# A decoder layer on one core: the first batch's output projection moved wholly into the loop

## What is computed

```
proj = layernorm(x) @ W_in.T ; u, gate = split(proj)          # 2048 channels each
u = silu(conv4(u) + conv_b) ; dt, B, C = rmsnorm parts of u @ Wx.T
delta = softplus(dt @ Wdt.T + dt_bias)
for t: state = exp(delta_t*A)*state + (delta_t*u_t)*B_t ; y_t = sum_n(state*C_t)   # 16 states n
y = (y + u*D) * silu(gate)
x = x + y @ W_out.T
```

## Time and profile before

| | us |
|---|---|
| median of 3 runs (lowest, highest) | 1678.84 (1677.64, 1682.73) |
| the profiled execution: its own time | 1682.06 |
| its span | 1680.3 |
| DVE busy | 1314.7 (78%) |
| PE busy | 1413.9 (84%), modelled |
| mean granted TensorE clock | 0.937 of 2.4 GHz |

### The profile page before, as it was taken

How to read it: one execution, slowest core, us unless ns; L and a number is a source line. 1 busy time by engine, 2 the same in 40 slices (tenths; PEclk the granted TensorE clock), 3 DMA queues, 4 the chain that set the end, 5 groups by cost and what they waited for, 6 DMA issues and landing times. The chain is left out here.

```text
span 1680.3 us, 17931 instructions
## 1 busy us (share of the span) xinstructions
PE 1413.9 (84%) x5576; PEld 730.5 (43%) x5576; DVE 1314.7 (78%) x1633; ACT 934.4 (56%) x1378; POOL 936.9 (56%) x771
## 2 busy tenths in 40 slices
PE   6998677788888987768798788888989994999798
PEld 3443234444444453344454454444434442444443
DVE  6586698898898889989998898889147556777684
ACT  1211567767767755877767767755233222556670
POOL 0000778798797877889988898797100000333200
PEclk9999798999998999977999999999999996999899
DMA  7596233442443423343673682674473103589504
GB/s 273 201 346 260 76 132 103 152 163 100 155 157 107 166 84 119 98 141 101 224 246 113 229 279 86 227 231 157 149 284 145 61 25 95 135 190 195 113 0 175
DMA packets 155468, 264.38 MB, mean 157 GB/s; under 512 B 76560, under 2 KB 94096, under 8 KB 149552
## 3 DMA queue, kind: packets, MB, share of 16 engines
q1 hardware_dynamic: 151056, 236.27, 43.7%
q10 hardware_dynamic: 4320, 27.00, 4.5%
HBM read 207.60 MB, written 38.60 MB: 147 GB/s over the span
## 5 line engine op out<-in xcount | busy, mean ns | idle before, releaser
L1047 DVE TENSOR_TENSOR_SCAN hbuf<-decay,hbuf 128x512 f32<-128x512 f32 x512 | 611.7, 1211 | 51.6 <-ACT decay L763 51.6
L763 ACT ACTIVATE decay<-delta,chan_sb 128x512 f32<-128x512 f32 x512 | 348.7, 687 | 293.1 <-DVE hbuf L1047 291.9
L579 PE MATMUL turn<-ident,hbuf 128*128 128x128 f32 x2048 | 337.9, 294 | 179.3 <-DVE hbuf L1047 137.6
L579 PEld LDWEIGHTS turn<-ident,hbuf 128*128 128x128 f32 x2048 | 256.3, 150 | 451.2 <-DVE hbuf L1047 213.7
L1061 DVE SCALAR_TENSOR_TENSOR acc<-turn,pn,acc 128x512 f32<-128x512 f32 x360 | 263.0, 731 | 40.4 <-PE turn L579 39.6
L893 POOL TENSOR_TENSOR hbuf<-du,sx 128x512 f32<-128x512 f32 x172 | 213.1, 1273 | 1.3 <-DMA sx<-bt_scratch 1.3
L893 POOL TENSOR_TENSOR hbuf<-wout,sx 128x512 f32<-128x512 f32 x172 | 213.6, 1278 | 0.4 <-POOL wout L903 0.2
L914 POOL TENSOR_TENSOR acc<-acc,part 128x512 f32<-128x512 f32 x120 | 153.3, 1278 | 52.5 <-ACT part L773 52.3
L1742 PE MATMUL bank<-codes,wout 128*128 128x512 bf16 (+1 forms) x704 | 153.8, 382 | 1.0 <-PEq L1156 1.0
L561 PE MATMUL bank_g<-wout,codes 128*128 128x512 f32 x256 | 139.8, 634 | 2.4 <-DVE wout L993 2.4
L493 PE MATMUL bank_u<-wout 128*128 128x512 f32 x224 | 113.1, 625 | 2.9 <-DMA wout<-in_wu 2.0
(11 more groups left out here) (212 smaller groups left out, 2124.0 us busy)
## 6 DMA issues: line engine op xcount, KB each, us to landing
wout<-in_woutT SPq DMA_DIRECT2D x48, 512.0 KB, 4.3
sx<-bt_scratch SPq DMA_DIRECT2D x86, 256.0 KB, 3.6
codes<-in_wg SPq DMA_DIRECT2D x8, 2048.0 KB, 8.9
ubuf<-u_scratch SPq DMA_DIRECT2D x16, 1024.0 KB, 6.1
wout<-in_w_gate SPq DMA_DIRECT2D x26, 512.0 KB, 4.7
wout<-in_w_up SPq DMA_DIRECT2D x26, 512.0 KB, 4.1
raw_d<-in_w_down ACTq DMA_DIRECT2D x8, 1376.0 KB, 7.4
b_more<-bt_scratch SPq DMA_DIRECT2D x42, 256.0 KB, 3.4
```

The costliest lines, as they stand in the source:

```text
L579: last = pe.transpose(turn[t % 2][:, j * P:j * P + P], hbuf[:, s % 4, j, t * P:t * P + P], ident[:, :])
L763: act.activation(decay_bank[q % 2][:, :], delta[:, G % 2, j, :], ACT.Exp, scale=a_col(GD * (G % GROUPS) + j, n)).then_inc(dA_done, 1)
L1047: dve.tensor_tensor_scan(h, decay_bank[q % 2][:, :], h, 0.0, ALU.mult, ALU.add).then_inc(scan_done, 1)
```

## The change

Tile w of the projection runs in group 4+w rather than 5+w, so all four tiles are in the loop and `wout_last`, the last `wout_copy` and its stores go. In groups 5 to 7 the chunks keep their steps (two in each of 0 to 7), with another w. In group 4 the 16 chunks stand in steps 9 to 14, as 2, 3, 3, 2, 3, 3, and ACT copies them out at the end of step 15. To make room, the gate products of group 4 move from steps 8 to 15 (four in each) to steps 2 to 8 (five in each, two in the last), and their copies from the steps (11, 13, 15, 16) to (3, 5, 6, 8). The weights of the gates are asked for in step 0 rather than 1.

```diff
+        def wout_chunks(G, n):
+            if G < GROUPS:
+                return range(0)
+            if G > GROUPS:
+                return range(2 * n, 2 * n + 2) if n < 8 else range(0)
+            i = n - 9
+            return range(DC * i // 6, DC * (i + 1) // 6) if 0 <= i < 6 else range(0)
+
+        def wout_copied(G, n):
+            return G == GROUPS and n == 15 or G > GROUPS and n == 9
...
-            lo, per = (9, 3) if G == 0 else (5, 3) if G == GROUPS - 1 else (8, 4)
+            lo, per = (9, 3) if G == 0 else (5, 3) if G == GROUPS - 1 else (2, 5) if G == GROUPS else (8, 4)
...
-            at = (-1, -1, 13, 15) if G == 0 else (9, 12, 14, 16) if G == GROUPS - 1 else (11, 13, 15, 16)
+            at = (-1, -1, 13, 15) if G == 0 else (9, 12, 14, 16) if G == GROUPS - 1 else \
+                (3, 5, 6, 8) if G == GROUPS else (11, 13, 15, 16)
... SP
-                    if n == 1 and G >= 1:
+                    if n == (0 if G == GROUPS else 1) and G >= 1:
                         load_wg(G)
...
-                    if b == 1 and g >= 1 and n < 8:
-                        if n == 0:
-                            load_yT(g - 1)
-                        for q in (2 * n, 2 * n + 1):
-                            load_w(BATCH * DC + DC * (g - 1) + q)
-                    if b == 1 and g >= 1 and n == 9:
+                    for c in wout_chunks(G, n):
+                        if c == 0:
+                            load_yT(g)
+                        load_w(BATCH * DC + DC * g + c)
+                    if wout_copied(G, n):
                         for half in range(2):
-                            store_attn(g - 1, half)
+                            store_attn(g, half)
...
-                        load_yT_last()
...
-            for half in range(2):
-                store_attn(TT - 1, half)
-            for i in range(2):
-                sp.wait_ge(yT_stored[i], 16 * (GD * NG // 2))
-            sp.wait_ge(attn_stored, 32 * TT)
+            for part in range(3):
+                sp.wait_ge(wout_in[part], 16)
... PE
-                            pe.wait_ge(wout_evac, 2 * (G - GROUPS))
+                            pe.wait_ge(wout_evac, 2 * (G - GROUPS + 1))
...
-                        pe.wait_ge(gate_evac, TT * (GROUPS + w + 1))
+                        pe.wait_ge(gate_evac, TT * (GROUPS + max(w, 1)))
...
-                        if b == 1 and g >= 1 and n < 8 and t % 2 == 1:
-                            wout_part(g - 1, 2 * n + t // 2, 2 * n + t // 2 + 1)
+                        w = wout_chunks(G, n)
+                        wout_part(g, w.start + len(w) * t // TT, w.start + len(w) * (t + 1) // TT)
...
-            wout_last(KC, DC)
             for j in range(GD):
                 turn_y(NG - 1, j)
-            wout_last(0, KC)
... ACT
-                    if b == 1 and g >= 1 and n == 9:
-                        wout_copy(g - 1)
+                    if G > GROUPS and wout_copied(G, n):
+                        wout_copy(g)
...
                     for j in gate_copies(G, n):
                         gate_copy(G, j)
+                    if G == GROUPS and wout_copied(G, n):
+                        wout_copy(0)
...
-            wout_copy(TT - 1)
```

More of the change, by code:

```diff
@@ L98, in mixer @@
         o_stage = [xT[:, 4, 0:L], xT[:, 5, 0:L]]
-        yT_last = [delta[:, 0, c // 4, (c % 4) * P:(c % 4) * P + P] for c in range(DC)]
         skip_diag = [soft[:, j // 2, (j % 2) * P:(j % 2) * P + P] for j in range(GD)]
-        o_last = [soft[:, half, :] for half in range(2)]
         x_view = [hbuf[:, i // 2, 2 * (i % 2):2 * (i % 2) + 2, :].rearrange("p a t -> p (a t)")
@@ L203, in mixer @@
         EARLY_GATE = 2
-        WOUT_BESIDE = GROUPS - 1
+        def wout_chunks(G, n):
[7 more added lines that the diff above has]
+            return G == GROUPS and n == 15 or G > GROUPS and n == 9
         UNITS = 2 * OC
@@ L346, in store_y @@
                     .then_inc(yT_stored[i % 2], 16)
[L348 to L352, removed]
             def load_yT(w):
@@ L366, in store_attn @@
                 sp.dma_start(attn_dram[w * P:w * P + P, half * 512:half * 512 + 512],
-                             (o_stage if w < WOUT_BESIDE else o_last)[half])\
+                             o_stage[half])\
                     .then_inc(attn_stored, 16)
@@ L438, in _ @@
                         sp.wait_ge(q_step, 4 * UNITS)
-                        sp.wait_ge(w_used, BATCH * DC + DC * WOUT_BESIDE)
+                        sp.wait_ge(w_used, BATCH * DC + DC * TT)
                         sp.wait_ge(dbu_done, GD * N * (NG - 1))
                         load_wout(KC, DC, 0)
-                        load_yT_last()
             sp.wait_ge(gate_mm, TT * NG)
-            sp.wait_ge(attn_stored, 32 * WOUT_BESIDE)
+            sp.wait_ge(attn_stored, 32 * TT)
             load_wout(0, KC // 2, 1)
@@ L609, in wout_part @@
                                          start=(c == 0), stop=(c == DC - 1))
[L610 to L624, removed]
                     last.then_inc(w_used, 1)
@@ L800, in wout_copy @@
             def wout_copy(w):
-                act.wait_ge(w_used, BATCH * DC + (DC * (w + 1) if w < WOUT_BESIDE else DC * w + 1))
+                act.wait_ge(w_used, BATCH * DC + DC * (w + 1))
                 if w >= 1:
@@ L804, in wout_copy @@
                 for half, bank in enumerate((bank_u, bank_s)):
-                    o = (o_stage if w < WOUT_BESIDE else o_last)[half]
-                    act.activation(o, bank[:, :], ACT.Copy).then_inc(wout_evac, 1)
+                    act.activation(o_stage[half], bank[:, :], ACT.Copy).then_inc(wout_evac, 1)
             for i in range(TT):
```

## The result

| | before | after |
|---|---|---|
| median of 4 runs each (us) | 1678.48 | 1698.08 |
| lowest, highest | 1677.64, 1682.73 | 1696.14, 1710.12 |
| ratio, with its 95% interval | | 1.0123 (1.0085 to 1.0161) |
| the profiled execution: time, span | 1682.06, 1680.3 | 1698.34, 1696.6 |
| mean granted TensorE clock | 0.937 | 0.931 |

The kernel is 19.6 us slower. The direction was right, but the projection in groups 4 and 5 was priced too low, and the gain at the end too high.

What follows compares the result with a forecast made beforehand. DVE was taken to pace the loop and PE the mixer's end; end -13.4, copies +10.3, ring +7.5, group 5's start +1.8, PE's clock +1.5 made +7.7 us: 1689.8 profiled, 1686.5 by the median, range 1674 to 1698.

Steps and rivals of the forecast that it cites:

- the gain at the end: After the loop: without wout_last's products the next block starts earlier, -13.4 us, between -15.4 and -10.
- The ring: Group 4: W_out chunks in two places, each turning in 6.2 us, finish late; +7.5 us, bounds +1.5 and about +17.
- the order on SP: Start of group 5: yT and first chunk loads stand behind tile 0's stores; +1.8 us, between 0 and +4.
- PE's own work: Group 4's three-chunk steps: four turns and six products, 7.0 us, alone cost about half a us each.
- The copies: Group 4: ACT's gate bank copies wait for PE and delay decays; +10.3 us in sum, between +5 and +13.
- Bank 2: Step 4.7: the copy delays decays and a softplus, so the next step begins 11.3 after the start, not 7.2; +4.1.
- bank 0: Group 4: PE's step 3 starts 1.3 late and the copy holds the scan 2.3 more; +3.6 us.
- bank 3: Group 4: copy and decay end 6.5 into the step against 3.9, with a softplus in that step too; +2.6 us.
- the rival at 1700: Group 4: PE's waits keep it at 1.2 GHz through the three-chunk steps, two such costing 14 more; 1700, chance 0.15.
- The no-change rival: Group 4: the ring turns within the steps, so its +7.5 goes unpaid; +0.2, 1679; chance 0.18.
- The faster rival: The end keeps 15.4, copies cost at most 5, loads land in about 3.4; -9, 1670; chance 0.15.
- the signs named: Profile after: ACT's gate waits, long steps 4.7 and 4.9, PE's W_out waits, group 4 130 to 135, end 27 not 42.

Runs made afterwards that it cites:

- e12: e3 with 14 of tile 0's 32 products left out and all chunk loads kept; ratio 0.9905 to the kernel before.
- e2: The changed kernel with four places for the chunks of W_out instead of two; 1681.8 us.
- e3: The changed kernel with gate copies one step later, four W_out chunk places, and tile 0's stores behind group 5's first loads; 1664.6 us, ratio 0.9909.
- e5: The changed kernel with tile 0's two stores asked for behind group 5's loads of yT and first chunks; 1693.44 us.
- e4: The kernel before with only the gate part of the change (group 4's gate products and copies earlier), projection as before; 1690.27 us.
- e9: e3 with three unread products added behind the first and three behind the third turn of y after the loop; ratio 0.9928.
- e7: e3 with four banks and four places for y after the loop; 1659.65 us, ratio 0.9897.
- e10: e7 with the 4 MB of W_out at the end left out but for two blocks; tail 27.7 us, no total given.
- e11: e7 with the 4 MB of W_out asked for behind the four stores of y; tail 36.5 us, no total given.

## Why the prediction was wrong

**The step that failed** is the price of the projection in group 4 and at the start of group 5: +7.5 and +1.8 forecast, +15.5 measured. The ring and the order on SP are there, the one priced too high and the other too low; PE's own work was put at next to nothing.

- *PE's own work.* The step said that four turns and six products, 7.0, "alone would cost about half a us each", and then priced the ring. It left out the dt product that PE's steps 4.9 and 4.11 hold as well, and that no gap is left when every step is full. e12 shows 3.1 us of it. Another 1.7 goes from e2 to e3 (47.5 to 45.8, clock 0.90 to 0.96), all of it in steps 4.14 and 4.15; in 4.14 the clock was 0.77 in e2 and 1.00 in e3. That the clock is its whole cause is not shown, since e3 has two more edits. The sum by window would have said so: 35.2 of PE before, less the 24 gate products that leave (20.7), plus 27.6, is 42.1 in a stretch of 41.9; e3 shows 41.99 [its window above]. PE, not DVE, bounds those steps.
- *The ring.* Forecast +7.5 by a turn of 6.2, measured 3.7 (e2). The loads landed in 3.7 there, not in the 4.3 of the earlier trace rows, and PE waited for seven chunks in the stretch, 4.5 in all, in four of its steps 4.10 to 4.14 (not in 4.12) and not in all five. With 3.7 the formula gives 8 x 5.6 = 44.8 for 41.0, +3.8. So that +7.5 came near the +9.3 was luck: too much for the ring, next to nothing for PE.
- *Group 5.* The order on SP was named, and "about 4 us late, mostly beside ACT's silu" was wrong twice: 7.3 late, and nothing hid it. Step 5.1 lost 4.4 and step 5.0 1.8. e5 gives 3.2 of the 6.2 to the order; most of the rest goes when tile 0 ends in time as well (+0.7 in e3). This is the largest single miss, 4.4.

**The second miss** is the end: -13.4 forecast, -9.7 measured. "The other three follow at 2.70 each as now" carried over a distance that was measured at 2.4 GHz and with stores that landed in 2.3. It is 13.95 for the three and not 8.1, 5.9 more. With the clock up in the second turn the three still take 12.5 to 14.4 (e12, e9, e2), since the first store is late; with four banks and places, where neither counts, 2.9 (e7).

**The copies** were right: +10.3 forecast, +10.9 alone (e4), +13.2 in the profile of the whole change. Bank 2 came out at +4.2 (4.1 forecast), bank 0 at +4.0 (3.6) and bank 3 at +4.2 (2.6); with the gates alone it was 4.2, 3.6 and 3.4. Bank 3 was dearer with PE's clock down behind the wait in step 4.7 (1.92 a pair at 775.36); that this is the whole reason is not shown.

**The rivals.** The measured 1698 lies nearest to the rival at 1700, held at 0.15, but its reason did not happen: in steps 4.10 to 4.15 the clock was 0.91, not 0.5. The no-change rival took the ring for free; with the ring of four the kernel does come to 1.0015, but because groups 6 and 7 get 10 shorter: PE's own work, which no rival had at the full clock, is still there. The faster rival needed copies at 5 or less; they cost 10.9. The Trainium skill's estimate (DMA: Bandwidth & Descriptors, Anatomy of one DMA), 3.2 for such a load and by it a free ring, was weighed and set aside. The page gives its figures for DMAs issued by GpSimd, and these are issued by SP, so it did not quite bear on them. The median landing of 3.7 in that stretch lies between it and 4.3, and the ring cost 3.7 us and not nothing.

Of the signs named: ACT's waits for gate products 14.2 in steps 4.3, 4.6 and 4.8 (at least 6) yes; steps 4.7 and 4.9 at 11.3 and 11.8 (10 to 11) just over; PE's waits for W_out in five of the steps 4.10 to 4.14 no, in four; group 4 at 137.4 (130 to 135) over; groups 5 to 7 within 3 us no, group 5 took 6.3 more; the end 9.7 gained, under the 10 at which I called myself wrong.

## What to carry to other kernels

Before work is moved into a stretch that one engine bounds, add up what the *other* engine will do there, everything included, against the stretch's length: at 42 of 42 every delay is paid in full, and no price per step shows it. A distance read from the trace (a turn, a store) holds only for the clock and the queue it was read with, so ask what was busy then and what will be idle now. An experiment on the clock needs more than one execution on each side: e12 had by chance what e9 had by its edit. And when the first repairs turn a loss into a gain, run them on the old kernel too: half of this gain or more was there for the taking without the change.

## What the runs showed of the hardware

- The first 256 KB store of y, asked for 8.3 us behind 4 MB of loads on the same queue, landed after 6.2 to 7.9 (6.2 in e12, 7.4 in e9, 7.7 after the change, 7.9 in e2), and after 2.3 without them (e10). In the other order the 2 MB reload took 14.5, not 5.9 (e11). The Trainium skill says that each DMA engine takes the descriptors of one queue in ring order (DMA: Bandwidth & Descriptors, Queues, rings and completion order); both numbers agree with that.
- PE's granted clock was 0.50 from 1220 to 1230, with waits of 2.08 and 0.69 in that time, and a turn of y took 3.8. At 1.00, 2.4 GHz, it takes 2.0 (e9, e12). The same wait of 3.05 between the first two turns was followed by a turn at 1.2 GHz in e3 and at 2.4 in e2 and e12.
- The later blocks, unchanged, took 449.6 to 462.0 in the twelve experiments' profiles, so a difference of a few us in the total needs the stretch by stretch reading.
